# Weights laid out in the arrays as the engines use them, and a loop head put at slot 0 of TensorE's instruction blocks

## The reference, cut to what matters

```python
def step(carry, xy):                       # x: (2048, 256, 32), y: (2048, 256)
    xt, yt = xy
    st, err, gs, mem, h1, c1, h2, c2 = carry
    encoded = tanh(xt @ We + st @ Ue + be)                       # 24 wide
    new_state = tanh(einsum('bd,cds->bcs', xt, Wx)
                     + einsum('bs,cst->bct', st, Ws) + bk)       # 8 candidates of 32
    mem = concat([concat([encoded, err])[:, None], mem[:, :-1]]) # the last 20 entries of 25
    a = relu(mem.reshape(b, -1) @ enc_w1 + enc_b1)               # 64 wide
    agent_in = relu(a @ enc_w2 + enc_b2)                         # 16 wide
    h1, c1 = lstm_cell(agent_in, h1, c1, ...)                    # 16 wide
    h2, c2 = lstm_cell(h1, h2, c2, ...)
    gate = softmax(h2 @ gate_w + gate_b)                         # 8 wide
    theta = clamp01(mean(abs(mem[:, :10, -1])) * 2.5)
    gate = gate * theta + gs * (1 - theta)
    st = einsum('bc,bcs->bs', gate, new_state)
    pred = clamp01(st[:, -1]); err = pred - yt
    return (st, err, gate, mem, h1, c1, h2, c2), pred
```

## Time and profile before

| what | value |
|---|---|
| median of 3 runs | 5925.37 us (5924.08 to 5929.31) |
| profiled execution | 5930.65 us, span 5928.8 us |
| TensorE (PE), matmuls | 5535.1 us busy, 93% of the span |
| VectorE (DVE) | 4689.8 us, 79% |
| ScalarE (ACT) | 3831.1 us, 65% |
| GpSimd (POOL) | 1639.7 us, 28% |
| mean granted TensorE clock | 0.979 of full speed |

### The profile page before, as it was taken

How to read it: one execution, slowest core, us unless ns; L and a number is a source line. 1 busy time by engine, 2 the same in 40 slices (tenths; PEclk the granted TensorE clock), 3 DMA queues, 4 the chain that set the end, 5 groups by cost and what they waited for, 6 DMA issues and landing times.

```text
span 5928.8 us, 184458 instructions
## 1 busy us (share of the span) xinstructions
PE 5535.1 (93%) x67584; PEld 3438.4 (58%) x67584; DVE 4689.8 (79%) x12854; ACT 3831.1 (65%) x9217; POOL 1639.7 (28%) x3588
## 2 busy tenths in 40 slices
PE   4999999999999999999999999999999999999998
PEld 2555555555555555555555555555555555555555
DVE  5878887887887887788788788788878878878887
ACT  2666666666666666666666666666666666666665
POOL 1222222222222222222222222222222222222222
PEclk9999999999999999999999999999999999999999
DMA  2111111111111111111111111111111111111111
GB/s 45 30 26 30 27 30 27 30 28 28 27 29 27 30 30 27 30 27 30 27 30 27 30 27 30 27 30 27 30 27 30 27 30 27 30 27 30 27 30 37
DMA packets 313074, 172.28 MB, mean 29 GB/s; under 512 B 171368, under 2 KB 278132, under 8 KB 312452
## 3 DMA queue, kind: packets, MB, share of 16 engines
q1 hardware_dynamic: 308724, 162.02, 10.4%
q10 hardware_dynamic: 3728, 0.15, 0.0%
HBM read 73.73 MB, written 2.10 MB: 13 GB/s over the span
## 4 chain that ended last, share of the span: by engine, by line
PE 71%; ACT 13%; DVE 9%; issue 6%; ACTq 1%; DMA 0%; POOL 0%; POOLq 0%; DVEq 0%
PE chain L442 16%; PE a_ps L404 10%; PE a_ps L393 8%; PE cand_ps L373 7%; PE cand_ps L364 7%; PE chain L429 6%; ACT a_sb L568 6%; ACT gates L593 4%; PE chain L338 4%; PE a_ps L415 4%; PE chain L459 4%; DVE cell_in L769 4%; DVE added L755 3%; PE cand_ps L359 3%; ACT tanh_c L599 2%
## 5 line engine op out<-in xcount | busy, mean ns | idle before, releaser
L393 PE MATMUL a_ps<-hist,w_hist 125*64 125x512 f16 x12288 | 1745.0, 389 | 80.9 <-DMA w_hist<-enc_table 80.9
L846 DVE TENSOR_REDUCE state<-mixed 128x64 f32<-128x512 f32 x2048 | 1353.3, 682 | 36.4 <-issue 2.4
L586 ACT ACTIVATE cand<-cand_ps 128x512 f32<-128x512 f32 x2048 | 1154.2, 590 | 184.6 <-PE cand_ps L373 184.6
L442 PE MATMUL chain<-cell_in,cell_w 128*64 128x128 f32 x16384 | 1092.9, 276 | 0.7 <-ACT cell_in L576 0.5
L442 PEld LDWEIGHTS chain<-cell_in,cell_w 128*64 128x64 f32 x16384 | 887.9, 136 | 288.8 <-ACT cell_in L576 181.4
L593 ACT ACTIVATE gates<-chain 128x512 f32<-128x512 f32 x1024 | 611.4, 597 | 619.7 <-PE chain L442 619.7
L959 POOL TENSOR_TENSOR err_ring<-pred_now,ys 128x8 f32 x512 | 122.0, 238 | 3129.6 <-DVE pred_now L853 3129.6
L393 PEld LDWEIGHTS a_ps<-hist,w_hist 125*64 125x64 f16 x12288 | 671.4, 112 | 526.1 <-issue 117.1
L755 DVE SCALAR_TENSOR_TENSOR added<-gates 128x256 f32<-128x256 f32 x1024 | 435.5, 425 | 445.2 <-ACT gates L593 445.2
L599 ACT ACTIVATE tanh_c<-gates 128x128 f32<-128x128 f32 x1024 | 316.9, 310 | 689.7 <-DVE gates L761 689.7
L769 DVE SCALAR_TENSOR_TENSOR cell_in<-gates,tanh_c 64x128 f32<-64x128 f32 x2048 | 585.7, 286 | 164.5 <-ACT tanh_c L599 150.9
(11 more groups left out here) (82 smaller groups left out, 6708.4 us busy)
## 6 DMA issues: line engine op xcount, KB each, us to landing
x_sb<-in_x_l SPq DMA_DIRECT2D x260, 256.0 KB, 2.8
hist<-entry_parts SPq DMA_DIRECT2D x2048, 25.0 KB
w_hist<-enc_table SPq DMA_DIRECT2D x258, 128.0 KB, 2.3
y_rows<-in_y_l SPq DMA_DIRECT2D x260, 8.0 KB
ys<-in_y SPq DMA_DIRECT2D x1, 2048.0 KB
preds_out<-preds SPq DMA_DIRECT2D x1, 2048.0 KB, 7.6
cell_w<-in_lstm_whh ACTq DMA_DIRECT2D x16, 3.0 KB
cell_w<-in_lstm_whh ACTq DMA_DIRECT2D x16, 1.0 KB
```

What stands on the lines that cost most here:

```text
L393: nc.tensor.matmul(a_ps[g][ENC * half:ENC * half + ENC, :], w_hist[0:HROWS, w_slot(u), kk, wp, :], hist[0:HROWS, xp, k, at:at + 512], star ...
L442: last = nc.tensor.matmul(chain[g][rows, P * r:P * r + P], cell_w[c][:, hf, r, :], cell_in[c][:, g, hf, :], start=False, stop=True, skip_g ...
L586: ins = nc.scalar.activation(cand[:, g, q // 2, :, q % 2, :, :].rearrange("p h s c -> p h (s c)"), cand_ps[q][:, :].rearrange("p (h k) -> ...
L846: V.tensor_reduce(state[:, g, hf, 2 * pair:2 * pair + 2, :], mixed[:, pair, hf, :, :, :], AX, ALU.add)\
```

## The change

The host passes every weight as an array that already has the layout of its place in on-chip memory, zeros included. Each is loaded by one transfer: 7 on SyncE's queue (identity and columns among them) and one for the start errors, and 11 on ScalarE's, with `ys` as the last. VectorE's zeroing of the weight arrays goes; `hist` is zeroed by GpSimd. VectorE's preparation is split by three waits: the biases (`s_biases`), the encoder's table (`s_table`), and all other loads (`s_load`) only ahead of the cells' weights; it waits for GpSimd's zeros (`s_hist0`) ahead of `hist`.

```diff
+TENSOR_HEAD = 0
-        def run_phases(eng, phase, turn_start=None):
+        def run_phases(eng, phase, turn_start=None, head_slot=None):
-            with nc.Fori(0, LOOPS, engines=[eng.engine], hint_back_edge=True) as turn:
+            with nc.Fori(0, LOOPS, engines=[eng.engine], hint_back_edge=True, head_slot=head_slot) as turn:
-            run_phases(pe, phase, turn_start)
+            run_phases(pe, phase, turn_start, {pe.engine: TENSOR_HEAD})
         @block.sync
+            load(columns[:, :], columns_c)
+            sp.dma_start(bk_stage, w["bk"]).then_inc(s_biases, 16)
             load(ident[:, :], ident_c)
-            load(columns[:, :], columns_c)
-            load(indicator[:, :], ind_c)
-            load(gate[:, :, :, :], gate0.rearrange("(g j p) c -> p g j c", g=GROUPS, p=P))
+            load(w_we[:, :], w["we"])
+            load(w_ue[:, :], w["ue"])
+            load(w_x[:, :], w["wx"])
+            load(w_s[:, :], w["ws"])
+            sp.wait_ge(s_zero, 1)
...
-            load(ys[:, :, :], y.rearrange("(n p) t -> p n t", p=P))
-            sp.wait_ge(s_zero, ZEROED)
...
         @block.scalar
-            act.wait_ge(s_zero, ZEROED)
...
+            act.dma_start(enc1_stage, w["encoder"]).then_inc(s_table, 16)
+            act.dma_start(bias_stage[:, :, :].rearrange("r n b -> r (n b)"), w["biases"]).then_inc(s_biases, 16)
+            act.dma_start(gate_bias_stage[:, :], w["gate_b"]).then_inc(s_biases, 16)
             for n in range(2):
+                load(cell_w[n][:, :, :, :].rearrange("p h r b -> p (h r b)"), w[f"cell{n}"])
+            load(w_now[:, :, :].rearrange("p a b -> p (a b)"), w["now"])
+            load(w_enc2[:, :], w["enc2"])
+            load(gate_w[:, :, :].rearrange("p h c -> p (h c)"), w["gate_w"])
+            load(indicator[:, :], ind_c)
+            load(gate[:, :, :, :], gate0.rearrange("(g j p) c -> p g j c", g=GROUPS, p=P))
+            act.dma_start(ys[:, :, :], y.rearrange("(n p) t -> p n t", p=P)).then_inc(s_ys, 16)
         @block.vector
-            V.memset(staged[:, :], 0.0)
...
-            V.memset(hist[:, :, :, :].rearrange("p a k b -> p (a k b)").bitcast(FP32), 0.0).then_inc(s_prep, 1)
+            V.memset(share[:, :, :], 0.0).then_inc(s_prep, 1)
             dve.wait_ge(s_prep, 1)
-            dve.wait_ge(s_load, loads[0])
+            dve.wait_ge(s_biases, 16 * 3)
...
+            link(V.tensor_copy(cand_bias[:, :], bk_stage))
+            link(V.tensor_tensor(cand_bias_low[:, :], bk_stage, cand_bias[:, :], ALU.subtract))
...
+            dve.wait_ge(s_table, 16)
...
+            dve.wait_ge(s_load, loads[0])
...
+            dve.wait_ge(s_hist0, 1)
         @block.gpsimd
+            G.memset(hist[:, :, :, :].rearrange("p a k b -> p (a k b)").bitcast(FP32), 0.0).then_inc(s_hist0, 1)
             pool.wait_ge(s_ready, 1)
+            pool.wait_ge(s_ys, 16)
```

## The result

The changed kernel takes 5656.3 us, the median of 4 runs (5656.01 to 5656.78), where the kernel before takes 5927.1 us, now the median of 4 runs too. The ratio is 0.9543, 95% interval 0.9527 to 0.9560. The forecast was 5648 us, range 5628 to 5700. The profiled execution's span fell from 5928.8 to 5654.1 us, by 274.7.

A forecast was written before the change was run, and what follows sets the result against it. TensorE bounds the kernel, idling each turn for its loop head's code fetch, and starts late. 5930.65 - 225 (loop) - 55.4 (start) = 5650 us, or 5645 if the profiled excess goes; forecast 5648 us, range 5628 to 5700.

The forecast's parts named there:

- The loop's excess: TensorE's loop: 4.5 us a turn beyond its work, 2.9 gap and 1.6 slow clock; removing it gives -225 us.
- the undisturbed turn: TensorE's loop: ten items of 10.93 us each, 109.3 us a turn without the stall.
- the step down from the sum: Total: from 5650 to 5648 us, since the profiled execution's excess over the median might lie in its stalls, giving 5645.
- The cause: TensorE's loop head: hinted code fetch starts on entering the branch's block, only 0.3 us ahead; slot 0 gives it time.
- the fetch ahead: TensorE's loop, head at slot 0: block entered 7.6 us ahead of the branch, fetch needs at most 3.96 us.
- The second rival: TensorE's loop: hinted fetch replaces the sequential one, adding a stall at the eleventh block's entry; 6095 us, chance 0.02.
- The Trainium skill's rule: Code fetch: purely sequential prefetch, a taken branch to a block not held forces a fetch; loop term would be 0.
- The first rival: TensorE's loop: the stall stays despite the head's new slot; 5870 us, chance 0.13.
- The slow clock: TensorE behind each turn's gap: granted clock of 0.50 costs 1.6 us a turn and goes with the gap.
- The start: Ahead of the loop: first matmul at 25.5 us instead of 80.9, term -55.4 us, between -59 and -47.
- The two operations of double width: VectorE's preparation at the start: the candidates' bias at double width takes 1.9 us.
- The lock: Start: VectorE and GpSimd share ports exclusively; GpSimd's zeroing might be held back, some 2 us on top of the sum.

The follow-up runs named there:

- e1: Kernel before, with only TensorE's loop head put at slot 0: 5709.6 us, ratio 0.9632.
- e3: Changed kernel, head at slot 0, without the branch prefetch hint on TensorE's loop: 5866.7 us, ratio 0.9899.
- e4: Changed kernel with TensorE's loop head at slot 79, branch in slot 255, the last of its block: 5662.2 us, ratio 0.9551.
- e5: Changed kernel with TensorE's loop head at slot 80, branch in slot 0 of its block: 5872.9 us, ratio 0.9912.
- e9: Changed kernel with TensorE's loop head at slot 128, branch in slot 48 of its block: 5660.1 us, ratio 0.9548.
- e6: Changed kernel with TensorE's loop head at slot 110, branch in slot 30 of its block: 5876.4 us, ratio 0.9919.
- e7: Changed kernel with TensorE's loop head at slot 150, branch in slot 70 of its block: 5657.0 us, ratio 0.9550.
- e2: Changed kernel without the directive on TensorE's loop head, so weight layout and order of preparation alone: 5873.0 us, ratio 0.9908.

## Why the prediction was right, step by step

**The loop's excess** was put at 4.5 us a turn and is 4.38. That is 219 us in place of 225, and 6 of the 8.3 us between 5648 and 5656.3. The mis-sized number is the undisturbed turn: 109.3 us was worked out from six items inside a turn, and a whole turn without a stall takes 109.44. Most of the remaining 2 us is the step down from the sum, 5650, to 5648.

**The cause** was read rightly: e1 shows it to be worth 218 us alone, e3 that the hint must be there, e4 and e5 that the branch's distance behind its block's entry decides. The claim that the fetch ahead is 7 us early was too high, since the packet starts 5 us ahead of the branch (the last fetch of an execution at 587.7 us starts between 582 and 583):

```profile
L164 PEldq COMPARE_BRANCH  x1: 337/337/337, 587.7 to 587.7; - x1
...
q8 instruction: 1, 0.02, 7.9%
```

It did not matter with 1.9 to 2.9 us needed from the packet's start (e9). The branch costs its sequencer 0.35 us and not VectorE's 0.06, hidden as foretold by queued matmuls. The expectations of the experiments added a picture that was wrong, of a fetch partly hidden when the branch comes soon after the entry (e6, e7, e9).

**The second rival**, at a chance of 0.02, named what the hint does, and the harm that it priced did not come. The hinted fetch does take the place of the sequential one: 564 packets with the hint and 613 without it at slot 0. It costs nothing at the entry of the eleventh block, so 6095 us was far off. It costs 2.87 us once, at the loop's exit, and only where the branch is the last of its block (e4).

**The Trainium skill's rule** of purely sequential prefetch ("Runtime: NRT & Kernel Launch", "Instruction fetch mechanics") is what e3 shows without a hint. With a hint the trace differs, and the measurement decides: one packet less a turn, and none needed behind the branch. The first rival, 5870 us, is where e2, e3 and e5 lie, between 5867 and 5873.

**The slow clock** went with the gap, as foretold: its 1.5 us of the 4.4 a turn need no other cause, since the granted clock is 1.00 in the mean from 24.86 to 5636 us once TensorE does not stand still.

**The start** was put at -55.4 us and is -56.0, by errors that cancel; that it came so near is in part luck. The biases landed at 5.2 us and not at 8.5. But the first cast was held until 7.9 by GpSimd's zeroing, a cost that the sum had at 0, since for this operation it asked only whether the zeros would come in time (they did, at 7.66). The two operations of double width take 0.43 + 0.69 = 1.1 us, not 1.9. The table's 5.5 us came as said, the cells took 2.2 for 2.0, and the stretch from `hist` to the first matmul took 7.0 us, not 6.2. The 0.8 us lie between the issue of the history weights and the first matmul, 3.66 us where they were 2.83; `ys`, issued at 6.45, landed 16.3 us later, in the middle of it. The lock that the Trainium skill describes in "SBUF — State Buffer", "SBUF: two separate sides", I had priced at some 2 us and left out of the sum; the trace agrees with 2.25 us, on VectorE's side rather than on GpSimd's. GpSimd did not wait for `ys`.

## What to carry to other kernels

Where an engine stands still once a turn with no releaser, look at its code queue: if the fetch of the loop's head starts only behind the branch, count where the branch lies in its block (256 instructions fit all runs here). In this kernel the hint helped only when the branch is well behind its block's entry (48 slots were enough here, 30 were not), so an edit that shifts the branch by a slot can switch the stall on or off (79 and 80), and a fixed slot for the head protects from edits ahead of the loop. An edit in the loop needs the count again. Leave some instructions in the branch's block behind it too, or the exit pays (79). At a kernel's start, count the transfers and what VectorE waits for; and when work is moved to GpSimd, ask what it holds up on VectorE while it runs.

## What the runs showed of the hardware that was not expected

- The effect of a hint is not graded near the block's entry: branch in slot 0 or 30, 3.5 us; in slot 48, 0.65 us; in slot 70, 0.45 us; in slot 176, 0.35 us.
- The hint acts on the last turn as well: its packet takes the place of the block behind the loop, which cost 2.87 us of standing still where the branch was the last of its block.
- A VectorE cast of 128x512 took 2.68 us beside a GpSimd zeroing and 0.43 us without it, while VectorE's own zeroings ran at 0.48 us for 128x512 beside the same GpSimd instruction, as in the kernel before, where GpSimd did nothing.
- GpSimd zeroes 128x8192 in 6.92 us, VectorE in 6.88 us.
- VectorE's large zeroing starts 1.65 us after the one ahead of it in both kernels that have it there, with no releaser in the profile. The cause stays open.
